# A four-layer decoder on one core: at which results of the second mixture GpSimd takes the context norm's two powers

## The chip, the core and the metric

The kernel runs on one core of a Trainium2 chip. The metric is the device time of one launch in microseconds (us), the median of several runs. The core has TensorE (matrix products, written PE in the profile), VectorE (DVE), ScalarE (ACT), GpSimd (POOL), SyncE (SP), which issues most transfers, and 16 DMA engines. Each engine works its own list of instructions in order and waits on semaphores that the others raise.

## The reference, cut to what matters

Twelve residual sublayers follow each other: self-attention, cross-attention and a feed-forward part, in four layers. The change stands in the sixth, a mixture of 8 experts with two choices for each of the 1024 tokens, and concerns the eighth, whose context norm is worked out ahead of time in the sixth.

```python
x = x + _L1_ffn_ref(_layernorm(x, axis=-1), L1_ffn_gate_w, L1_ffn_w1, L1_ffn_w2, L1_ffn_w3)
x = x + _L2_attn_ref(_layernorm(x, axis=-1), L2_attn_Wqkv...)
x = x + _L2_xattn_ref(ctx_1024, mask_BxS2_bf1, _layernorm(x, axis=-1), L2_xattn_gm, L2_xattn_bm,
                      L2_xattn_gl, L2_xattn_bl, L2_xattn_Wq, L2_xattn_Wk, L2_xattn_Wv, L2_xattn_Wo)

def _layernorm(x, gamma, beta):          # of the eighth sublayer, for its context of 4 x 512 rows
    mu = jnp.mean(x, axis=-1, keepdims=True)
    var = jnp.var(x, axis=-1, keepdims=True)
    return (x - mu) * jax.lax.rsqrt(var + EPS) * gamma + beta
```

(The second line is abridged: its arguments are the sublayer's weights and biases.)

## The kernel before

**The mixture.** The tokens' choices are packed into 23 blocks of 128 rows, each with one expert. For every block b, TensorE makes the two up products (lines L1993 and L1995), ScalarE the SiLU of the first (L2064, tile `gated`), VectorE the product of both (L2260), TensorE the down product (L2006), and VectorE copies the result y(b) out of PSUM (L2267). In TensorE's list the down product of block b-1 stands behind the up products of block b. The up products of block b wait for VectorE's product of block b-2, and the down product of b-1 for that of b-1. So in VectorE's list, step b is: product of block b, copy of result b-1, and then, for b from 2 to 19, one step of the context's norm.

**The context's norm** is taken in two halves of 8 tiles of 128x128 (tile `qs`), nine steps each (`CTX_STEPS = 9`). Steps 0 to 3 take statistics, two tiles each; step 3 ends with `veps` (L3091). Step 4 is empty. Step 5 waits for `rstd`, which GpSimd makes from `veps` with one power (L279), and steps 5 to 8 scale two tiles each (L3097). The first half's veps comes in VectorE's step b = 5 and is wanted as rstd in its step b = 7; the second half's in b = 14, wanted in b = 16.

**GpSimd's list** in this mixture is short: eight gathers of token rows for blocks 4 to 11 (L2341, scr_h to the row buffer, which the profile calls `probs`), then for each b the scatter of result y(b) to DRAM (L2329, `scr_y`), behind it for b from 4 to 14 the gather for block b + 8, and at two values of b the power. The sizes that tie the engines are these: results have 8 buffers, and VectorE's copy of y(b), b from 8 on, waits until the scatter of y(b-4) has landed; rows have 8 buffers, two blocks a group, and TensorE turns a group (L1980) just ahead of the up products of the odd block before it. So TensorE turns blocks 12 and 13 ahead of block 11's up products.

**SyncE** loads an expert's weights (768 KB, L1784) into one of 5 buffers; the load for block b waits for the down product of block b-5. When all scatters have landed, it fetches the results back (L1801), and VectorE adds them to x (L2305). TensorE meanwhile starts on the eighth sublayer's keys (L2967 to L2983).

Of the kernel before, what the change touches and what calls it, by code (L numbers as in the profile page):

```python
# [79 lines left out]
def program(nc, a, ctx):  # L80
# [190 lines left out]
    def norm_gpsimd(pool, n, first=0):  # L271
        for part in range(first, parts_of(n)):
            power_gpsimd(pool, n, part)
# [85 lines left out]
    class Attention:  # L359
# [1172 lines left out]
        def gpsimd(self, pool):  # L1532
            for who, what, s, u in self.order():
                who.gpsimd_step(pool, what, s, u)
# [119 lines left out]
    CTX_STEPS = 9  # L1654

    class Mixture:
# [655 lines left out]
        def gpsimd(self, pool):  # L2312
            m = self.m
            if self.sorted:
                pool.wait_ge(placed.sem, placed.at(m, 2))
                pool.wait_ge(written, 16 * 7)
                for t in range(self.choices * NT):
                    pool.indirect_dma_start(scr_x, bass.IndirectOffsetOnAxis(ap=place[:, t:t + 1], axis=0),
                                            h[:, t % NT, :], None).then_inc(sorted_out.sem, 16)
                pool.wait_ge(mapped.sem, mapped.at(m, 1))  # L2320
            else:
                pool.wait_ge(h_spill.sem, h_spill.at(m, 4))
                pool.wait_ge(mapped.sem, mapped.at(m, 1))
                for b in range(self.turned_in * self.gb, self.turned_in * self.gb + RING):
                    self.gather_gpsimd(pool, b)
            pool.wait_ge(mapped.sem, mapped.at(m, 2))
            for b in range(self.nb):
                pool.wait_ge(y_sb.sem, y_sb.at(m, b + 1))
                pool.indirect_dma_start(scr_y, bass.IndirectOffsetOnAxis(ap=scatter_to[:, b:b + 1], axis=0),  # L2329
                                        yblk[:, self.at(b), :], None).then_inc(y_spill[b % 4].sem, 16)  # L2330
                if not self.sorted and self.turned_in * self.gb <= b < self.nb - RING:
                    self.gather_gpsimd(pool, b + RING)
                if m == 1 and b in (6, 6 + CTX_STEPS):
                    norm_gpsimd(pool, 7 + b // CTX_STEPS)

        def gather_gpsimd(self, pool, b):
# [1403 lines left out]
```

## Time and profile before

| | us |
|---|---|
| median of 3 runs | 1364.19 (1357.69 to 1368.22) |
| profiled execution | 1358.5 |
| its span, first to last instruction | 1356.7 |
| TensorE busy in the span | 1195.5 (88%) |
| VectorE | 898.5 (66%) |
| ScalarE | 733.3 (54%) |
| GpSimd | 272.9 (20%) |

The span is what the trace covers; the 1.8 us beside it lie before the first and after the last instruction. A share of busy time is a mean over twelve sublayers with different limits, so it doesn't tell what bounds one of them. All times in the rows are counted from the start of the span. The blocks of the changed mixture lie between about 462 and 535 us.

### The profile page before, as it was taken

The numbers are of one execution on the slowest core, as the hardware profiler recorded it, in microseconds if no ns is written. First come the engines' busy times: TensorE is split into PE (matmuls) and PEld (weight loads), VectorE is DVE, ScalarE is ACT, GpSimd is POOL, SyncE is SP. The second block draws the span as 40 slices with busy tenths as digits, with TensorE's granted clock in tenths as the row PEclk, the third lists the DMA queues.
The fourth block names the chain that finished last, engine by engine and source line by source line (L and its number), as shares of the span: only waits on it lengthen the run. The fifth ranks groups of instructions, "written<-read, shape, count | busy, mean of one in ns | idle before, by whom it ended". The sixth has DMA issues, their size and how long they took to land.

```text
span 1356.7 us, 26928 instructions
## 1 busy us (share of the span) xinstructions
PE 1195.5 (88%) x9641; PEld 723.5 (53%) x9641; DVE 898.5 (66%) x2346; ACT 733.3 (54%) x1501; POOL 272.9 (20%) x562
## 2 busy tenths in 40 slices
PE   5888999896887899669999999999988968989995
PEld 2334343793343598455666666666656833333333
DVE  4767995445767543776766676777746176777866
ACT  3565884232733323545666666676734535646674
POOL 2521220562010174210000000000005505212220
PEclk9898999998997899899999999999989989989997
DMA  7431238563412586300000000011116734211200
GB/s 175 114 72 46 57 122 325 202 219 119 116 41 74 186 278 205 124 1 1 1 1 1 1 1 1 9 33 47 40 42 210 251 125 108 62 48 50 54 9 16
DMA packets 90180, 121.69 MB, mean 90 GB/s; under 512 B 10977, under 2 KB 68014, under 8 KB 89070
## 3 DMA queue, kind: packets, MB, share of 16 engines
q1 hardware_dynamic: 84322, 110.40, 26.3%
q0 software_dynamic: 4096, 8.40, 1.9%
q8 instruction: 79, 1.29, 0.4%
q10 hardware_dynamic: 1632, 1.18, 0.3%
q14 instruction: 51, 0.42, 0.1%
HBM read 88.94 MB, written 30.02 MB: 88 GB/s over the span
## 4 chain that ended last, share of the span: by engine, by line
PE 65%; DVE 14%; ACT 5%; DMA 5%; issue 5%; POOL 3%; SPq 2%; DVEq 0%; ACTq 0%; POOLq 0%
PE ps L2910 7%; PE ps L2917 7%; PE ps L2925 6%; PE ps L1202 6%; PE ps L945 4%; PE ps L1993 3%; PE ps L2006 3%; PE ps L954 3%; PE ps L2999 3%; PE ps L3006 2%; PE ps L1995 2%; PE ps L1112 2%; PE ps L1239 2%; PE ps L231 2%; PE ps L1902 2%
## 5 line engine op out<-in xcount | busy, mean ns | idle before, releaser
L3117 DVE CUSTOM_DVE_ANT_0 wring<-ps,probs 128x768 f32<-128x768 f32 x128 | 122.6, 958 | 46.1 <-PE ps L2910 45.4
L3076 ACT COPY qs<-ps 128x768 f32<-128x768 f32 x128 | 102.3, 800 | 90.3 <-PE ps L2917 90.3
L1202 PE MATMUL ps<-probs,vaug 128*32 128x256 f32 (+1 forms) x1792 | 142.3, 392 | 5.0 <-issue 3.5
L1157 ACT ACTIVATE probs<-ps 128x512 f32<-128x512 f32 x192 | 104.2, 595 | 60.0 <-PE ps L998 59.8
L279 POOL TENSOR_TENSOR rstd<-veps,mhalf 128x4 f32<-128x4 f32 (+2 forms) x28 | 26.6, 949 | 514.6 <-DVE veps L247 501.3
L1030 DVE TENSOR_REDUCE mx<-ps 128x2 f32<-128x1024 f32 (+1 forms) x96 | 115.5, 1220 | 22.1 <-PE ps L945 21.2
L1161 ACT ACTIVATE probs<-ps 128x512 f32<-128x512 f32 x192 | 104.7, 594 | 39.2 <-PE ps L1112 38.0
L3057 ACT ACTIVATE wring<-wring,r 128x768 f32<-128x768 f32 x128 | 120.8, 944 | 3.9 <-DVE r L3120 3.9
L2917 PE MATMUL ps<-ident,wring 128*128 128x128 f32 x768 | 110.2, 280 | 3.2 <-DVE wring L3161 3.2
L2917 PEld LDWEIGHTS ps<-ident,wring 128*128 128x128 f32 x768 | 83.4, 140 | 41.9 <-issue 35.3
L2910 PE MATMUL ps<-probs 64*128 64x512 f32 (+1 forms) x512 | 100.4, 510 | 1.1 <-DVE r L3117 1.1
L2329 POOL DMA_INDIRECT scr_y<-probs x85 | 82.1, 966 | 70.2 <-DVE probs L2267 53.5
L1018 DVE CUSTOM_DVE_ANT_0 wring<-ps,m3x 128x512 f32<-128x512 f32 x128 | 83.2, 688 | 17.0 <-PE ps L945 9.7
L2925 PE MATMUL ps<-qs,ks 128*64 128x256 f32 x768 | 89.9, 383 | 0.0
L3161 DVE TENSOR_SCALAR wring<-wring,r 128x768 f32<-128x768 f32 x128 | 79.4, 621 | 4.5
L945 PE MATMUL ps<-ks,qs 49*128 49x256 bf16 (+1 forms) x512 | 76.9, 338 | 4.6 <-DVE mx L1030 1.8
L2260 DVE TENSOR_TENSOR probs<-gated,ps 128x256 f32<-128x256 f32 (+1 forms) x62 | 32.2, 520 | 58.6 <-ACT gated L2064 32.7
L2064 ACT ACTIVATE gated<-ps 128x256 f32<-128x256 f32 (+1 forms) x62 | 28.7, 463 | 76.6 <-PE ps L1995 76.6
L2910 PEld LDWEIGHTS ps<-probs 64*128 64x128 f32 x512 | 44.4, 187 | 47.6 <-issue 40.9
L2925 PEld LDWEIGHTS ps<-qs,ks 128*64 128x64 f32 x768 | 52.3, 137 | 28.4 <-issue 5.2
L1202 PEld LDWEIGHTS ps<-probs,vaug 128*32 128x32 f32 x1792 | 36.7, 109 | 52.2 <-issue 47.7
L1112 PE MATMUL ps<-qs,ks 52*128 52x256 bf16 x384 | 54.5, 281 | 4.7 <-DMA qs<-mT 2.9
(397 smaller groups left out, 2468.1 us busy)
## 6 DMA issues: line engine op xcount, KB each, us to landing
wring<-in_L_ffn_w SPq DMA_DIRECT2D x21, 768.0 KB, 5.5
wring<-in_L_ffn_w SPq DMA_DIRECT2D x19, 514.0 KB, 4.8
ks<-in_L_ffn_w SPq DMA_DIRECT2D x8, 768.0 KB, 14.5
qs<-in_L_ffn_w SPq DMA_DIRECT2D x6, 768.0 KB, 12.3
qs<-scr_q SPq DMA_DIRECT2D x18, 192.0 KB
qs<-scr_qx SPq DMA_DIRECT2D x16, 192.0 KB
probs<-scr_x SPq DMA_DIRECT2D x12, 256.0 KB, 5.4
probs<-in_L_ffn_w SPq DMA_DIRECT2D x4, 768.0 KB, 6.2
```

Of the source, the lines that this page charges most:

```text
L945: ins = pe.matmul(bank(at[r], i * self.keys, (i + 1) * self.keys), self.qv(s, c, r, ROWS_A, t * P, (t + 1) * P), self.kv(s, c, r, ROWS_A), ...
L1018: dve.tensor_tensor_reduce(wring[:, k % 2, r * S2:(r + 1) * S2], bank(self.banks(0, k)[r]), m3x[:, 0, a % 2 * S2:(a % 2 + 1) * S2], 1.0, - ...
L1030: dve.tensor_reduce(out, src, AX.X, ALU.max, negate=True).then_inc(a_max.sem, 1)
L1157: act.activation(probs[:, s % 2, 2 * c + r, kt0 * S:(kt0 + 2) * S], bank(self.banks(3, k)[r]), ACT.Exp).then_inc(p_exp.sem, 1)
L1161: act.activation(probs[:, s % 2, 2 * c + r, kt0 * S:(kt0 + 2) * S], bank(4 + k % 2), ACT.Exp).then_inc(p_exp.sem, 1)
L1202: ins = pe.matmul(ps[32 * j:32 * j + 32, self.av_bank(s), q0:S], vaug[:, s % 2, kt, j, :], probs[:, s % 2, j, at:at + S - q0], start=(kt = ...
L2910: ins = pe.matmul(bank(2 * j + lo // 512, 0, hi - lo), self.qT[rows, g % 2, k * P:(k + 1) * P], self.kT[rows, g % 3, lo:hi], start=True, s ...
L2917: ins = pe.transpose(self.buffer("turn", i, t * P, t * P + P), self.sc[:, i % 4, t * P:(t + 1) * P], ident[:, :])
L2925: ins = pe.matmul(self.buffer("sum", i, 0, S)[HW * j:HW * j + HW, :], self.v[:, i % 3, t, j * HW:(j + 1) * HW], self.pT[:, i % 2, j, t, :] ...
L3057: act.activation(self.sc[:, i % 4, :], self.sc[:, i % 4, :], ACT.Exp, bias=self.neg[:, i % 4:i % 4 + 1], accum_out=self.tot[:, i % 4:i % 4 ...
L3076: act.copy(self.pT[:, g % 2, j, :, k * P:(k + 1) * P], self.buffer("turn", i, 0, KV).rearrange("p (t n) -> p t n", n=P)).then_inc(self.out ...
L3117: dve.tensor_tensor_reduce(self.sc[:, s, :], src, self.maskb[:, u // (2 * PR), :], 1.0, -3.0e38, ALU.add, ALU.max, self.top[:, s:s + 1]).t ...
```

## The change

One line sets after which results GpSimd takes the two powers. Results are counted here from the first, y(0): the power of the first half moves from behind y(6) to behind y(3), that of the second half from behind y(15) to behind y(13).

```diff
                 if not self.sorted and self.turned_in * self.gb <= b < self.nb - RING:
                     self.gather_gpsimd(pool, b + RING)
-                if m == 1 and b in (6, 6 + CTX_STEPS):
+                if m == 1 and b in (3, 4 + CTX_STEPS):
                     norm_gpsimd(pool, 7 + b // CTX_STEPS)
```

`norm_gpsimd(pool, 7)` and `norm_gpsimd(pool, 8)` issue one power each:

```python
pool.wait_ge(ln_var.sem, ln_var.at(made(n), part + 1))
pool.tensor_tensor(rstd[:, at], veps[:, at], mhalf[:, at], ALU.pow).then_inc(ln_rstd.sem, 1)
pool.wait_ge(ln_rstd.sem, ln_rstd.at(made(n), part + 1))
```

No instruction is added or removed, and only GpSimd's list differs. Its first piece, at the head of the mixture's blocks (L2341 is a gather, L2329 a scatter of a result, L279 with 128x8 a power of the context's norm):

```order
 L2341 DMA probs<-scr_h,probs 128x128 x8
-L2329 DMA scr_y<-probs 7041x128 x5
-L2341 DMA probs<-scr_h,probs 128x128
-L2329 DMA scr_y<-probs 7041x128
-L2341 DMA probs<-scr_h,probs 128x128
-L2329 DMA scr_y<-probs 7041x128
-L2341 DMA probs<-scr_h,probs 128x128
+L2329 DMA scr_y<-probs 7041x128 x4
 L279 TENSOR_TENSOR rstd<-veps,mhalf 128x8
 L2329 DMA scr_y<-probs 7041x128
```

The power now stands behind four scatters in place of seven scatters and three gathers: the scatters of y(4), y(5), y(6) and the gathers for blocks 12, 13 and 14 come after it. The second piece, on GpSimd too, near the end of the blocks:

```order
 L2341 DMA probs<-scr_h,probs 128x128
 L2329 DMA scr_y<-probs 7041x128
+L2341 DMA probs<-scr_h,probs 128x128
+L2329 DMA scr_y<-probs 7041x128
+L2341 DMA probs<-scr_h,probs 128x128
 L279 TENSOR_TENSOR rstd<-veps,mhalf 128x8
-L2329 DMA scr_y<-probs 7041x128 x7
+L2329 DMA scr_y<-probs 7041x128
+L2341 DMA probs<-scr_h,probs 128x128
+L2329 DMA scr_y<-probs 7041x128 x8
```

Here the second power stands ahead of the scatters of y(14) and y(15) and of the last gather, for block 22, in place of behind them. (The plus lines above the power are those that the first power's move put behind it.)

## Rows read from the trace of the kernel before

**Rows 1.** The page: the span, and the chain that ended last, by engine.
```profile
span 1356.7 us, 26928 instructions
...
PE 65%; DVE 14%; ACT 5%; DMA 5%; issue 5%; POOL 3%; SPq 2%; DVEq 0%; ACTq 0%; POOLq 0%
```

**Rows 2.** Timeline of VectorE: start, length, instruction, and idle time before it.
```profile
481.51 0.17 DVE L3091 TENSOR_SCALAR veps<-mv 128x8 f32<-128x8 f32 x1
482.45 0.69 DVE L2260 TENSOR_TENSOR probs<-gated,ps 128x512 f32<-128x512 f32 x1 [0.77 <-ACT gated L2064]
...
492.01 0.60 DVE L3097 TENSOR_SCALAR qs<-qs,mv,rstd 128x128 f32<-128x128 f32 x2 [5.77 <-POOL rstd L279]
...
511.46 0.38 DVE L3091 TENSOR_SCALAR veps<-mv 128x8 f32<-128x8 f32 x1
...
519.18 0.60 DVE L3097 TENSOR_SCALAR qs<-qs,mv,rstd 128x128 f32<-128x128 f32 x2 [2.99 <-POOL rstd L279]
```

**Rows 3.** Timeline of TensorE in the mixture's blocks.
```profile
473.08 0.44 PE L1980 MATMUL ps<-ident,probs 128*128 128x128 f32 x2 [0.44 <-DMA probs<-scr_h,probs]
...
488.02 0.38 PE L1980 MATMUL ps<-ident,probs 128*128 128x128 f32 x2
...
493.26 1.62 PE L2006 MATMUL ps<-wring,probs 128*128 128x128 f32 x8 [3.07 <-DVE probs L2260]
```

**Rows 4.** Timeline of ScalarE: the SiLU of blocks 7, 8, 9, 10, 18, 19.
```profile
484.65 0.60 ACT L2064 ACTIVATE gated<-ps 128x512 f32<-128x512 f32 x1 [1.42 <-PE ps L1995]
487.33 0.60 ACT L2064 ACTIVATE gated<-ps 128x512 f32<-128x512 f32 x1 [2.08 <-PE ps L1995]
...
490.23 0.60 ACT L2064 ACTIVATE gated<-ps 128x512 f32<-128x512 f32 x1 [1.41 <-PE ps L1995]
497.87 0.60 ACT L2064 ACTIVATE gated<-ps 128x512 f32<-128x512 f32 x1 [7.04 <-PE ps L1995]
...
520.18 0.60 ACT L2064 ACTIVATE gated<-ps 128x512 f32<-128x512 f32 x1 [2.08 <-PE ps L1995]
...
523.63 0.60 ACT L2064 ACTIVATE gated<-ps 128x512 f32<-128x512 f32 x1 [1.42 <-PE ps L1995]
```

**Rows 5.** Timeline of GpSimd: two norms' powers, then scatters, a gather, the powers.
```profile
391.75 1.01 POOL L279 TENSOR_TENSOR rstd<-veps,mhalf 128x4 f32<-128x4 f32 x1 [0.37 <-DVE veps L247]
...
477.70 1.00 POOL L2329 DMA_INDIRECT scr_y<-probs  x1 [0.30 <-issue]
...
481.58 0.97 POOL L2329 DMA_INDIRECT scr_y<-probs  x1 [0.30 <-issue]
...
489.28 0.98 POOL L2341 DMA_INDIRECT probs<-scr_h,probs  x1 [0.30 <-issue]
490.29 1.68 POOL L279 TENSOR_TENSOR rstd<-veps,mhalf 128x8 f32<-128x8 f32 x1
...
517.47 1.68 POOL L279 TENSOR_TENSOR rstd<-veps,mhalf 128x8 f32<-128x8 f32 x1
```

**Rows 6.** Stretches: busy us by engine, then TensorE's granted clock, DMA share, GB/s.
```profile
493.20:497.20 4.00, 3.94 (x20) 3.94 (x21) 2.11 (x8) 0.00 (x0) 2.42 (x3) 0.57 0.23 46
...
472.50:476.50 4.00, 3.06 (x26) 2.71 (x25) 1.61 (x6) 0.79 (x2) 2.89 (x4) 1.00 0.84 210
...
479.00:488.00 9.00, 9.00 (x83) 9.00 (x82) 3.58 (x11) 2.76 (x5) 6.86 (x7) 1.00 1.01 342
503.00:527.00 24.00, 23.71 (x212) 23.52 (x211) 11.92 (x38) 6.86 (x13) 15.09 (x15) 1.00 0.95 306
```

**Rows 7.** DMA issues at 489.28, 516.47, 486.26, 495.63, 516.22: us to landing.
```profile
probs<-scr_h,probs POOLq DMA_INDIRECT x1, 4.6
...
scr_y<-probs POOLq DMA_INDIRECT x1, 6.7
...
wring<-in_L_ffn_w SPq DMA_DIRECT2D x1, 768.0 KB, 5.2
...
wring<-in_L_ffn_w SPq DMA_DIRECT2D x1, 768.0 KB, 4.6
...
wring<-in_L_ffn_w SPq DMA_DIRECT2D x1, 768.0 KB, 7.6
```

## The prediction

> **What bounds the kernel now.** I read the page's chain of waits first. TensorE holds 65% of the chain that ended last, and GpSimd only 3% [rows 1]; but the kernel is a row of sublayers, and one of them can hang on an engine that is idle elsewhere. So the second view is the timeline of the changed mixture, engine by engine. VectorE has its first veps ready at 481.51 + 0.17 = 481.68, and yet sits idle 5.77 us, up to 492.01, for the rstd made of it; the second time it idles 2.99 us, up to 519.18 [rows 2]. Why so late? GpSimd comes out of its eight gathers with four results already waiting and works without a pause from then on: from 477.70 to 489.28 lie nine intervals, so one transfer costs its queue 1.29 us. It reaches the power only at 490.29, 8.6 us after its input was there [rows 5, 2].
>
> Third, what the wait costs where it matters. VectorE's product of block 8 stands behind the waiting step. TensorE idles 3.07 us for it, then starts at 493.26 with a down product of 1.62 us, and in the stretch around it the granted clock is 0.57 on average, against 1.00 before [rows 3, 6]: after the idle time it works at the lower of its two levels (1.2 GHz of 2.4) for a while. The whole loss is best read on ScalarE, whose SiLU marks the end of each block's up products. Undisturbed they are 2.68 and 2.90 us apart in turn (487.33 - 484.65, 490.23 - 487.33), 5.58 us for two blocks. Block 10 should come at 490.23 + 2.68 = 492.91 and comes at 497.87 [rows 4]. **The first wait costs the chain 4.96 us**, some 3.2 as idle time and 1.7 as slow clock. The second wait: block 19 comes 3.45 us after block 18 (523.63 - 520.18) where 2.90 is the pace [rows 4]. **It costs 0.55 us**, since most of its 2.99 lie in VectorE's slack. Between and after them TensorE sets the pace of the blocks.
>
> **The change part by part.**
>
> *The first power, behind y(3).* GpSimd starts that scatter at 481.58 and is done at 482.55 [rows 5]; veps is there since 481.68, so the power doesn't wait, with 0.9 us to spare. It runs from 482.58 to 484.26 (1.68, the same shape as before [rows 5]). VectorE asks for rstd at 492.01 - 5.77 = 486.24 [rows 2], 2.0 us later: the wait of 5.77 is gone, and with it the loss of 4.96.
>
> *What is queued behind it.* y(4) is next. A power that waits for its own semaphore before the next instruction shows a gap of 0.37 [rows 5], so y(4) is issued at 484.63, against 481.58 + 1.29 = 482.87 before: 1.76 later. The gather of block 13 stands three transfers behind: 484.63 + 3 x 1.29 = 488.5. TensorE turned the group of blocks 10 and 11 at 488.02 [rows 3]; the group of 12 and 13 follows two blocks later, at 488.02 + 5.58 = 493.6, since TensorE no longer stops. The gather has 5.1 us to land. Its nearest neighbour, issued at 489.28, took 4.6; the slowest of GpSimd's transfers in these rows 6.7 [rows 7]. I take 4.6, thus no wait; the other end is 488.5 + 6.7 - 493.6 = 1.6 us. Each later group gains room, since two transfers a block cost GpSimd 2.58 us and a block lasts 2.79. VectorE's copy of y(8), at about 491.5, needs the scatter of y(4): 484.63 + 4.6 to 6.7 is 489.2 to 491.3, just in time, nothing.
>
> *The second power, behind y(13).* After the first power GpSimd lags: y(7), the fourth scatter from y(4) with three gathers between, goes at 484.63 + 6 x 1.29 = 492.4 and y(13), twelve transfers on, at 507.8; the gather behind it ends at 510.1, and the power at about 511.8. Its veps came at 511.46 + 0.38 before, now 4.96 us earlier, at 506.9. VectorE wants rstd at 519.18 - 2.99 - 4.96 = 511.2 [rows 2]. It still waits 0.6 us, well inside its slack (a wait of 2.99 cost 0.55), so the 0.55 us go too. The scatters of y(14) and y(15) and the last gather are some 2 us later than they would be; from y(16) on there are only scatters, GpSimd catches up, and the last one is issued when its result is copied, as before.
>
> *What is late next: the transfers.* A block moves 768 KB of weights and 64 KB each in and out, 0.9175 MB in 2.79 us, 329 GB/s. With the engines fully busy they moved 342 [rows 6]: little is left over. The stop of TensorE let them drain: the load issued after it landed in 4.6 us, the one before it had taken 5.2, and ten undisturbed blocks later, at 516.22, one took 7.6 [rows 7]. Block 20's up products end at 523.63 + 2.68 = 526.31 and take 1.99 (read from the undisturbed blocks: the SiLU at 490.23 follows the turn at 488.02 by 2.21, the turn itself 0.22), so its weights were wanted at 524.3, 8.1 us after the issue. Without the second stop that is 7.55. Without the first stop's pause the landing would be 0.6 longer (5.2 against 4.6), 8.2. I charge the difference, **0.6 us**. The ends: nothing, by the 342 GB/s, and 2.1 us by the 306 GB/s of the later stretch [rows 6]: ten blocks, 9.175 MB, in 30.0 us in place of 27.9.
>
> The Trainium skill ("DMA: Bandwidth & Descriptors", Where 436 GB/s comes from) puts the limit of HBM for one core at about 358 GB/s. By it the blocks' demand would always fit, and the sum would be the full 5.5; the trace is less generous, with landings that grow while the share stands near 1.
>
> *After the mixture* everything hangs on the last block: the scatters, the fetch back, the add to x and the next norm follow in a chain, and TensorE's work on the next keys starts when its blocks end. I find no transfer or engine there that runs on its own clock, so what is saved stays saved.
>
> **The sum:** -4.96 - 0.55 + 0.6 = **-4.9 us**. The profiled execution took 1358.5 us (a span of 1356.7 and 1.8 around it) and would take 1353.6. The median of the runs shown is 5.7 us above that execution; from it, 1364.2 - 4.9 = **1359.3 us**, 0.4% less.
>
> **The rivals.**
>
> *The transfers take most of it back.* For it: the share near 1 and the landings of 6.7 and 7.6. Against it: the waits overlap (what TensorE loses at the turn it doesn't lose again at the weights), and the ring of five weight buffers has 2 us of room. With both ends, 1.6 at the turn and 2.1 at the weights, 1.8 us of gain are left: 1362.4; in the middle, 1361.
>
> *The power is held up at its new place.* Both powers of before ran while VectorE stood idle; now VectorE has a product of 0.69 us from 482.45 on [rows 2]. If the power can't run beside it, the power and all behind it come up to 0.6 us later, the gather of block 13 at 489.1 lands at 493.7 to 495.8, and up to 2.2 us are lost at the turn: from -4.8 to -3.3, middle 1360. The Trainium skill ("SBUF — State Buffer", Who interferes with whom) has such a rule: a VectorE instruction with two SBUF inputs and a GpSimd instruction that reads SBUF exclude each other. This product reads one input from PSUM, so the rule speaks only weakly here.
>
> *It does nothing.* If the end of the mixture hung on something that the trace's waits don't name, the time would stay: 1364.2. TensorE's idle time names VectorE's product, and that product stands directly behind the wait; I see little room.
>
> *Slower.* GpSimd's list is strict, and three gathers now stand behind the power. If the gather of block 13 landed so late that TensorE idled over 3.8 us at the turn, the clock would fall as it did after 3.07 us and cost 1.7 more, and the sum turns positive. That needs a landing of 8.9 us or more; at 10 us it is 4.9 + 1.7 - 5.5 = +1.1, 1365.3. The slowest of GpSimd's transfers in the rows took 6.7 [rows 7]. A short idle alone doesn't lower the clock: it stayed at 1.00 around the 0.44 us before 473.08 [rows 3, 6].
>
> **How the numbers follow.** The forecast 0.65 (-5.5 to -4.0), transfers 0.18, held power 0.06, nothing 0.06, slower 0.02, and 0.03 for more than forecast, should later stretches at the lower clock fall shorter. About 1% is what a measurement of this kernel can tell from no change; it is 13.6 us here, and no case reaches it by its mechanism. What is left for the other two is scatter: the three runs lie within 10.5 us. Faster by over 1% 0.05, within 1% 0.93, slower 0.02. The mechanisms span 1358.7 to 1364.2; half the scatter, 5.3, to either side makes 1353.4 to 1369.5. The profiled execution as the basis gives a time 5.7 lower, so I move the range down: 1350 to 1366.
>
> **What the changed profile would show.** VectorE's first L3097 with no wait on rstd, and the second with under 1 us; the SiLUs of blocks 8 to 22 at 2.68 and 2.90 throughout, and no granted clock of 0.5 around 495; the first 128x8 power near 482.6; block 19's SiLU near 518.1 (523.63 - 5.51) or up to 0.6 later. It would be wrong if TensorE waited for rows at the turn near 493.6 or for weights from block 16 on, if the power waited for veps, or if the mixture ended 5 us earlier and a later sublayer gave it back.

## The result, and the profile after

The changed kernel takes 1358.66 us (median of 22 runs, 1349.83 to 1364.93), against 1368.3 us for the kernel before in 22 runs beside it. The ratio is 0.995, with a 95% interval of 0.9929 to 0.9972: 0.5% faster, or 7 us of some 1366. The profiled execution took 1362.48 us with a span of 1360.7.

That span is 4.0 us longer than that of before [rows 1], so the page alone would mislead. Its first line and its chain by engine:

```profile
span 1360.7 us, 26923 instructions
...
PE 66%; DVE 13%; DMA 6%; ACT 5%; issue 5%; POOL 2%; SPq 2%; DVEq 0%; ACTq 0%; POOLq 0%
```

GpSimd's share of the chain went from 3 to 2%, that of the transfers from 5 to 6%. To see what the change did, the two traces have to be laid side by side at the mixture. ScalarE's SiLU of block 0 starts at 464.15 before and at 468.17 here: 4 us have been lost ahead of the change, in sublayers that it doesn't touch. I therefore count every kernel from block 0's SiLU to block 22's. **That stretch took 67.63 us before and takes 63.22 now, 4.41 less.**

The timeline of VectorE in the changed kernel (start, length, instruction, idle time before it), to be read beside [rows 2]:

```profile
485.30 0.17 DVE L3091 TENSOR_SCALAR veps<-mv 128x8 f32<-128x8 f32 x1
486.24 0.69 DVE L2260 TENSOR_TENSOR probs<-gated,ps 128x512 f32<-128x512 f32 x1 [0.77 <-ACT gated L2064]
...
489.94 0.59 DVE L3097 TENSOR_SCALAR qs<-qs,mv,rstd 128x128 f32<-128x128 f32 x2
...
516.24 0.79 DVE L3097 TENSOR_SCALAR qs<-qs,mv,rstd 128x128 f32<-128x128 f32 x2
```

Neither of the two L3097 that follow a power has idle time any more, where 5.77 and 2.99 us stood. GpSimd's timeline, beside [rows 5]:

```profile
485.58 0.97 POOL L2329 DMA_INDIRECT scr_y<-probs  x1 [0.30 <-issue]
486.57 1.69 POOL L279 TENSOR_TENSOR rstd<-veps,mhalf 128x8 f32<-128x8 f32 x1
488.55 1.02 POOL L2329 DMA_INDIRECT scr_y<-probs  x1 [0.29 <-POOL rstd L279]
...
492.47 0.98 POOL L2341 DMA_INDIRECT probs<-scr_h,probs  x1 [0.30 <-issue]
...
514.01 1.68 POOL L279 TENSOR_TENSOR rstd<-veps,mhalf 128x8 f32<-128x8 f32 x1
```

The first power begins 1.1 us after its veps and ends at 488.26, before VectorE asks. The gather of block 13 goes out at 492.47. ScalarE's SiLUs of blocks 9, 10, 11 and of 18, 19, beside [rows 4]:

```profile
494.02 0.60 ACT L2064 ACTIVATE gated<-ps 128x512 f32<-128x512 f32 x1 [1.41 <-PE ps L1995]
496.70 0.60 ACT L2064 ACTIVATE gated<-ps 128x512 f32<-128x512 f32 x1 [2.08 <-PE ps L1995]
...
500.90 0.60 ACT L2064 ACTIVATE gated<-ps 128x512 f32<-128x512 f32 x1 [1.41 <-PE ps L1995]
...
520.32 0.60 ACT L2064 ACTIVATE gated<-ps 128x512 f32<-128x512 f32 x1 [2.08 <-PE ps L1995]
...
523.21 0.60 ACT L2064 ACTIVATE gated<-ps 128x512 f32<-128x512 f32 x1 [1.42 <-PE ps L1995]
```

Block 9 to 10 is 2.68 us (7.64 before), block 18 to 19 is 2.89 (3.45 before). But block 10 to 11 is 4.20, where 2.90 is the pace: 1.30 us are new. TensorE's timeline and two stretches (busy us by engine, granted clock, DMA share, GB/s) say what they are:

```profile
498.64 0.44 PE L1980 MATMUL ps<-ident,probs 128*128 128x128 f32 x2 [1.09 <-DMA probs<-scr_h,probs]
```
```profile
493.20:497.20 4.00, 4.00 (x38) 4.00 (x38) 1.44 (x5) 1.10 (x2) 3.09 (x4) 1.00 0.96 328
...
497.00:500.00 3.00, 1.91 (x17) 1.73 (x17) 1.40 (x4) 0.67 (x2) 2.26 (x3) 1.00 0.97 314
```

TensorE waits 1.09 us for the token rows of blocks 12 and 13 at their turn. The granted clock stays at 1.00 through it (0.57 in the stretch 493.20:497.20 of [rows 6]), and no other turn and no load of weights is waited for from there on. So the balance is -4.96 - 0.56 + 1.30, and -0.19 of small differences at blocks 3 to 5 and beyond: -4.41.

### The profile page after: what moved, and what is told of

Same layout as the page of the kernel before. It is cut to its first block, busy times and chain, and to the rows that moved or that the text cites. A ratio compares the mean times of both kernels' runs of the same rounds, so it can differ in the third digit from the quotient of the medians.

```text
span 1360.7 us, 26923 instructions
## 1 busy us (share of the span) xinstructions
PE 1201.9 (88%) x9636; PEld 727.5 (53%) x9641; DVE 898.9 (66%) x2346; ACT 734.4 (54%) x1501; POOL 271.5 (20%) x562
## 4 chain that ended last, share of the span: by engine, by line
PE 66%; DVE 13%; DMA 6%; ACT 5%; issue 5%; POOL 2%; SPq 2%; DVEq 0%; ACTq 0%; POOLq 0%
PE ps L2910 7%; PE ps L2917 7%; PE ps L2925 6%; PE ps L1202 6%; PE ps L945 4%; PE ps L1993 3%; PE ps L2006 3%; PE ps L954 3%; PE ps L2999 3%; PE ps L3006 2%; PE ps L1112 2%; PE ps L1995 2%; PE ps L231 2%; PE ps L1239 2%; PE ps L1902 2%
## 5 line engine op out<-in xcount | busy, mean ns | idle before, releaser
L279 POOL TENSOR_TENSOR rstd<-veps,mhalf 128x4 f32<-128x4 f32 (+2 forms) x28 | 26.6, 949 | 519.4 <-DVE veps L247 506.0
L2329 POOL DMA_INDIRECT scr_y<-probs x85 | 81.9, 964 | 67.2 <-DVE probs L2267 47.5
```

## The experiments

Each was read in two ways: by the stretch from block 0's to block 22's SiLU in its trace, which differs by 0.06 to 0.24 us in the three kernels that were traced twice, and by its runs against the kernel before, whose intervals are 6 to 10 us wide in all. The stretch is one trace each, so differences of a few tenths say nothing.

| kernel | blocks 0 to 22, us | ratio to before | 95% interval |
|---|---|---|---|
| before | 67.63 | | |
| before again (e10) | 67.40 | 1.0016 | 0.998 to 1.0052 |
| changed | 63.22 | 0.995 | 0.9929 to 0.9972 |
| changed again (e5) | 63.28 | 0.9952 | 0.9926 to 0.9978 |
| first power alone (e1) | 64.00 | 0.9985 | 0.9962 to 1.0009 |
| second power alone (e2) | 67.38 | 1.0005 | 0.9979 to 1.0031 |
| norm steps two blocks later (e3) | 62.11 | 0.9956 | 0.9932 to 0.9981 |
| the same again (e11) | 62.35 | 0.9923 | 0.9891 to 0.9956 |
| one more power (e4) | 64.71 | 0.9983 | 0.9959 to 1.0007 |
| two more powers (e8) | 65.12 | 0.9994 | 0.9969 to 1.0019 |
| gather ahead of scatter (e6) | 64.27 | 0.9945 | 0.9916 to 0.9974 |
| first power behind y(5) (e7) | 62.85 | 0.9956 | 0.9927 to 0.9984 |
| lighter loads (e9) | 61.41 | 0.9933 | 0.9902 to 0.9965 |

**e1: only the first power moves** (from the kernel before).

```diff
-                if m == 1 and b in (6, 6 + CTX_STEPS):
+                if m == 1 and b in (3, 6 + CTX_STEPS):
```

> Only the power of the first half moves, behind y(3); the second stays behind y(15). My theory: VectorE's first wait (5.77 us) is gone and TensorE's stop and slow clock of 4.96 us with it, TensorE waits about 1.1 us at the turn of blocks 12 and 13, as in the changed kernel, and at the second power GpSimd's backlog costs VectorE a wait of 2 to 4 us, of which 0.4 to 1.5 us reach TensorE. From block 7 to block 22, ScalarE's SiLUs take 3.0 to 4.0 us less than before. Rival, that the gain needs both moves: the second wait grows by as much as the first shrank, and the mixture ends within 1.5 us of before.

The blocks take 64.00 us, 3.63 less than before. VectorE's one wait for rstd, and TensorE's two waits:

```profile
520.47 0.60 DVE L3097 TENSOR_SCALAR qs<-qs,mv,rstd 128x128 f32<-128x128 f32 x2 [3.23 <-POOL rstd L279]
```
```profile
499.56 0.44 PE L1980 MATMUL ps<-ident,probs 128*128 128x128 f32 x2 [0.93 <-DMA probs<-scr_h,probs]
...
521.72 1.16 PE L2006 MATMUL ps<-wring,probs 128*128 128x128 f32 x8 [0.53 <-DVE probs L2260]
```

The first wait is gone without the second move; the second is 3.23 us in place of 2.99 and lets block 19 come 0.79 us late. The rival is out. The wait for rows at 499.56 belongs to the first move.

**e2: only the second power moves.**

```diff
-                if m == 1 and b in (6, 6 + CTX_STEPS):
+                if m == 1 and b in (6, 4 + CTX_STEPS):
```

> Only the power of the second half moves, behind y(13). My theory: the first wait stays at 5.5 to 6 us with its slow clock, the second goes from 3.0 to under 0.7 us, and the blocks gain 0.4 to 0.7 us. Rival, that most of the 8 us between the two kernels' runs comes from the second half or from a later sublayer that wants it early: a gain of 2 us or more.

67.38 us, 0.25 less than before, where 0.4 to 0.7 were expected; of the two waits for rstd one is left. VectorE, and TensorE's down product behind it:

```profile
486.69 0.60 DVE L3097 TENSOR_SCALAR qs<-qs,mv,rstd 128x128 f32<-128x128 f32 x2 [6.15 <-POOL rstd L279]
```
```profile
487.94 2.08 PE L2006 MATMUL ps<-wring,probs 128*128 128x128 f32 x8 [3.45 <-DVE probs L2260]
```

Block 18 to 19 is 2.90 here, so the 0.55 us are won. Block 19 to 20, at 3.10, gives 0.4 back: TensorE waits for the weights of block 20.

```profile
518.63 0.49 PE L1993 MATMUL ps<-probs,wring 128*128 128x128 f32 x2 [0.16 <-DMA wring<-in_L_ffn_w]
```

The first wait costs 0.25 us more than in the trace of before. The second move does what it should and weighs little, and nothing large hides in it.

**e10: the kernel before, again.**

> The kernel before, once more, for its scatter: the runs differ from the kernel before itself by nothing beyond their interval, VectorE waits 5.5 to 6.3 us for the first rstd and 2.8 to 3.3 for the second, and the blocks take 67.2 to 68.0 us. Rival, that the first wait is often far longer than in the profile shown, which would explain a difference of 8 us between the runs: over 69 us.

The same two waits as in [rows 2 and 3], 5.92 and 2.99 us, and 67.40 us in all; the ratio to itself, 1.0016, shows what the runs can tell:

```profile
494.57 0.60 DVE L3097 TENSOR_SCALAR qs<-qs,mv,rstd 128x128 f32<-128x128 f32 x2 [5.92 <-POOL rstd L279]
521.55 0.60 DVE L3097 TENSOR_SCALAR qs<-qs,mv,rstd 128x128 f32<-128x128 f32 x2 [2.99 <-POOL rstd L279]
```

The rival, a first wait that is often far longer, has no support: three traces with the power behind y(6) show 5.77, 5.92 and 6.15 us.

**e5: the changed kernel, again.**

> The changed kernel once more, beside the next three. From block 0's to block 22's SiLU the traces gave 67.63 us before and 63.22 changed, 4.41 less, while the means of the two kernels' runs lay 8.2 apart. My theory: the blocks are all that changed and the rest is scatter; here the blocks take 62.9 to 63.6 us, TensorE waits 0.7 to 1.5 us for rows at the turn of blocks 12 and 13, and the runs lie 3 to 7 us under those of before. Rival, that a later sublayer gains too: 8 us or more again.

63.28 us, with 1.11 us of waiting for rows at the same turn. The means of the runs lie 5.5 us apart (standard error 1.3), against 8.2 (1.35) in the first comparison: together 6.8, with a standard error of 0.9. The rival, 8 us or more again, has no support.

**e3 and e11: leave the powers, move who asks.** From the kernel before, VectorE takes the norm's steps two blocks later.

```diff
-                if m == 1 and 2 <= b < 2 + 2 * CTX_STEPS:
-                    others[7].context_vector(dve, *divmod(b - 2, CTX_STEPS))
+                if m == 1 and 4 <= b < 4 + 2 * CTX_STEPS:
+                    others[7].context_vector(dve, *divmod(b - 4, CTX_STEPS))
```

> Both powers stay where they were, behind y(6) and y(15), and VectorE takes its eighteen steps of the context's norm two blocks later (b from 4 to 21). Both rstd are then made when VectorE asks for them. My theory (the changed kernel's wait at the turn comes from GpSimd's list, which issues the gather of block 13 1.8 us later): no wait of VectorE over 0.4 us, the gather of block 13 goes 2.6 us ahead of that of block 14 and TensorE waits under 0.3 us at its turn; the blocks take 5.2 to 5.8 us less than before, about 1.1 less than changed. Rival, that the full transfer engines make that wait, whatever GpSimd does: TensorE waits 0.8 us or more at that turn or at a neighbouring one, and nothing is won against the changed kernel.

62.11 us, 5.52 less than before, and the gap of every block from 4 on is 2.68 to 2.99. One wait of 0.20 us for rstd is left, and no turn is waited for:

```profile
495.76 0.60 DVE L3097 TENSOR_SCALAR qs<-qs,mv,rstd 128x128 f32<-128x128 f32 x2 [0.20 <-POOL rstd L279]
```

> VectorE's norm steps two blocks later, once more. The first time the blocks took 62.11 us with no wait at any turn or for weights. My theory (the gather of block 13 has room when it stands ahead of the power): 62.0 to 62.6 us again. Rival, that this was luck with the transfer engines, which cost the kernel with the gathers ahead of the scatters 2.2 us in waits for weights: over 63 us.

62.35 us; nothing at the turn of blocks 12 and 13 this time either, only 0.42 us between blocks 7 and 8. Those 0.42 us are a wait for the weights of block 8. Against the two traces of before, the two of this kernel give 5.1 to 5.5 us by another way than the changed one. At the same pace of the blocks, its gather of block 13 goes out 6.9 us ahead of the turn (5.1 in the changed kernel) and lands after 4.9, so the pace as such doesn't make the 1.3 us.

**e7: the first power behind y(5) and its gather** (from the changed kernel).

```diff
-                if m == 1 and b in (3, 4 + CTX_STEPS):
+                if m == 1 and b in (5, 4 + CTX_STEPS):
```

> The first power behind y(5) and its gather, the second behind y(13) as in the changed kernel. The gathers of blocks 12 and 13 then go out before the power. My theory: VectorE waits 2.6 to 3.4 us for rstd, of which its slack hides all but 0.3 to 0.8, and TensorE doesn't wait at the turn: 62.4 to 62.9 us for the blocks, better than changed. Rival, that the wait at the turn isn't tied to the order of gather and power: it is there as well, and the blocks take over 63.6.

62.85 us, 0.4 under the changed kernel. VectorE waits, TensorE less, and there is no wait for rows:

```profile
495.10 0.60 DVE L3097 TENSOR_SCALAR qs<-qs,mv,rstd 128x128 f32<-128x128 f32 x2 [3.55 <-POOL rstd L279]
```
```profile
496.35 1.16 PE L2006 MATMUL ps<-wring,probs 128*128 128x128 f32 x8 [0.85 <-DVE probs L2260]
```

Both the wait and its cost are above what was expected (2.6 to 3.4 us, and 0.3 to 0.8). 3.55 us of waiting cost 1.12 at the next block (3.80 against 2.68), where 5.77 cost 4.96: the price of this wait is far from proportional. VectorE's slack hides a part, and the granted clock stayed at 1.00 after the stop of 0.85.

**e6: the gather ahead of the scatter** (from the changed kernel).

```diff
+                if not self.sorted and self.turned_in * self.gb <= b < self.nb - RING:
+                    self.gather_gpsimd(pool, b + RING)
                 pool.indirect_dma_start(scr_y, ...)
-                if not self.sorted and self.turned_in * self.gb <= b < self.nb - RING:
-                    self.gather_gpsimd(pool, b + RING)
```

> The changed kernel, with GpSimd's gather for block b + 8 ahead of the scatter of y(b) in place of behind it. My theory: the gather of block 13 is issued 1.3 us earlier, TensorE's wait at the turn falls from 1.1 to under 0.3 us, and the blocks take 62.0 to 62.5 us against 63.2; the scatter of y(4) is 1.3 us later and may hold VectorE's copy of y(8) by up to 0.5 us. Rival, that loaded transfer engines make the wait: it stays at 0.8 us or more.

The wait for rows is gone, as my theory had it, but the blocks take 64.27 us: TensorE waits for the weights of blocks 8, 19 and 20.

```profile
484.33 0.49 PE L1993 MATMUL ps<-probs,wring 128*128 128x128 f32 x2 [0.93 <-DMA wring<-in_L_ffn_w]
...
515.80 0.49 PE L1993 MATMUL ps<-probs 128*128 128x128 f32 x2 [0.41 <-DMA probs<-in_L_ffn_w]
...
519.23 0.49 PE L1993 MATMUL ps<-probs,wring 128*128 128x128 f32 x2 [0.49 <-DMA wring<-in_L_ffn_w]
```

The waits sum to 1.83 us, and these three blocks come 2.6 us later than at the pace. The size expected was missed by 1.8 us. The stop at block 8 also gave the gather of block 13 another 1.2 us; since it landed after 5.1 us, it would have been in time without it. It can't be said from one trace whether the new order made these waits: e4 waits 1.34 us for block 8's weights too, and of the two traces of the same kernel, e3 and e11, only the second does.

**e4 and e8: hold up GpSimd more** (from the changed kernel). One or two further powers behind the first, on a spare tile. The edit of e4:

```diff
                     norm_gpsimd(pool, 7 + b // CTX_STEPS)
+                if m == 1 and b == 3:
+                    pool.tensor_tensor(spare_pow[:, :], mhalf[:, :], mhalf[:, :], ALU.pow)
```

> The changed kernel with one more power of 128x8 on GpSimd, right behind the first one, whose result nobody reads: it holds up GpSimd's list by some 1.7 us and VectorE not at all. My theory: the gather of block 13 lands that much later, TensorE's wait at the turn grows from 1.1 to 2.6 to 3.0 us, the later groups wait too or get by with little room, and the blocks take 1.5 to 2.0 us more than in the changed kernel. Rival, that the wait is made by the transfer engines: it stays within 0.7 us of 1.1. If the clock falls after that wait as it did after 3.07 us, another 1 to 1.7 us are lost.

64.71 us, 1.49 over the changed kernel. But the wait at the turn, expected at 2.6 to 3.0 us, is as before, and 1.34 us went elsewhere:

```profile
489.32 0.49 PE L1994 MATMUL ps<-probs,wring 128*128 128x128 f32 x2 [1.34 <-DMA wring<-in_L_ffn_w]
...
498.85 0.44 PE L1981 MATMUL ps<-ident,probs 128*128 128x128 f32 x2 [1.01 <-DMA probs<-scr_h,probs]
```

(Lines are one further down in this kernel.) The wait for weights comes first and covers the delay, so this kernel alone decides nothing. Hence the doubling:

> The changed kernel with two further powers of 1.63 us behind the first one, whose results nobody reads: GpSimd's list is held up by 3.3 us more than in the changed kernel. With one such power a wait of 1.34 us for weights stood ahead of the turn and hid what it did there. My theory: the waits of TensorE for rows and those that come from VectorE's copies waiting for scatters sum to 1.1 + 3.3 = 4.4 us, give or take 0.8; if one of them is over 3 us the granted clock falls to about half and 1 to 1.7 us are lost besides. The blocks take 66.5 to 68.5 us, as many as before the change. Rival, that the list has room: they take under 65.

65.12 us, against 66.5 to 68.5 expected. GpSimd's extra powers, the gather of block 13, and then TensorE's and VectorE's waits:

```profile
487.18 3.23 POOL L2338 TENSOR_TENSOR spare_pow<-mhalf 128x8 f32<-128x8 f32 x2
...
494.51 0.97 POOL L2345 DMA_INDIRECT probs<-scr_h,probs  x1 [0.31 <-issue]
```
```profile
498.70 0.44 PE L1981 MATMUL ps<-ident,probs 128*128 128x128 f32 x2 [1.33 <-DMA probs<-scr_h,probs]
```
```profile
495.79 0.29 DVE L2268 COPY probs<-ps 128x128 f32<-128x128 f32 x1 [0.57 <-DMA scr_y<-probs]
498.58 0.29 DVE L2268 COPY probs<-ps 128x128 f32<-128x128 f32 x1 [0.68 <-DMA scr_y<-probs]
```

**Here my theory fell.** Counted from block 0's SiLU, the gather of block 13 went out 3.2 us later than in the changed kernel. TensorE came to the turn 1.0 us later, for stops that lie ahead of the extra powers, and waited only 0.2 us longer. The gather landed 4.2 us after its issue; in the changed kernel TensorE could go on 6.2 us after it (492.47 to 498.64). So the wait isn't GpSimd's lateness passed on. What GpSimd's transfers did in the changed kernel shows in four single microseconds, from 492, 493, 495 and 496 on (queue, packets, MB, time of its packets as a share of 16 engines):

```profile
q1 hardware_dynamic: 55, 0.33, 88.3%
q0 software_dynamic: 3, 0.00, 1.1%
...
q1 hardware_dynamic: 63, 0.31, 75.4%
q0 software_dynamic: 32, 0.08, 20.6%
...
q1 hardware_dynamic: 58, 0.36, 93.3%
...
q1 hardware_dynamic: 57, 0.28, 92.5%
q0 software_dynamic: 41, 0.09, 23.1%
```

q0 is GpSimd's queue, q1 that of the weights. In the microsecond from 495 on no packet of GpSimd moves at all, though two of its transfers are on their way; then 41 in the next. Rows come in bursts among the weights.

**e9: the changed kernel with a third of the weights left out.**

```diff
+                w = 1024 if m == 1 and b >= WS else n
-                sp.dma_start(wslot[b % WS][:, 0:n], self.packed[bass.ds(expert, 1), :, :]...
+                sp.dma_start(wslot[b % WS][:, 0:w], self.packed[bass.ds(expert, 1), :, 0:w]...
```

> The changed kernel, but from block 5 on only the first two thirds of an expert's weights are loaded (512 KB in place of 768; the down products use what an earlier expert left, so this part of the computation is left out). GpSimd's list is as in the changed kernel. The traces so far: TensorE waits 1.1 to 1.3 us at the turn of blocks 12 and 13 whether the gather of block 13 goes out as in the changed kernel, 1.7 or 3.3 us of queue later, and GpSimd's packets run in bursts between the weights'. My theory now: the gather has to get past the weights in the transfer engines, and its lateness only decides in which burst it goes. With a third of the weights gone it lands in under 4.5 us, the wait at the turn is under 0.2 us, and the blocks take 61.7 to 62.2 us. Rival, that GpSimd's lateness alone makes the wait: it stays at 0.8 us or more.

61.41 us, 0.3 less than expected, and block 10 to 11 is 2.94: 1.26 of the 1.81 us against the changed kernel are won there, and 0.52 between blocks 3 and 4. GpSimd's list stands as in the changed kernel (the gather of block 13 at 492.62); its DMA issue, and a stretch of the blocks:

```profile
probs<-scr_h,probs POOLq DMA_INDIRECT x1, 4.3
```
```profile
484.00:496.00 12.00, 12.00 (x110) 12.00 (x109) 6.11 (x20) 3.13 (x6) 9.55 (x10) 1.00 0.77 240
```

With the DMA engines 77% busy the gather lands in 4.3 us and TensorE doesn't wait. All traces together, for the gather of block 13 (room is from its issue until TensorE comes to the turn):

| kernel | room, us | landing, us | wait, us |
|---|---|---|---|
| changed, e5, e1 | 5.1 to 5.3 | 6.1 to 6.2 | 0.93 to 1.11 |
| e4 | 5.1 | 6.1 | 1.01 |
| e8 | 2.9 | 4.2 | 1.33 |
| e9 | 4.4 | 4.3 | none |
| e3, e6, e7, e11 | 6.9 to 7.7 | 4.9 to 5.3 | none |

The wait came wherever the room was about 5 us or less at full loads, and was absent in each of the four traces with 6.9 us or more. What sets the landing time is only partly shown. e9 says fewer weights, but in e8 the gather landed in 4.2 us with the DMA engines 94% busy meanwhile, and in e4 in 6.1 with 87%. So e9 can owe its 4.3 us to its lighter loads or to where the gather fell among them. One thing the traces do show. A transfer's semaphore is raised in 16 steps. In each of the four traces that took 6.1 to 6.2 us, 15 of the 16 had come 5.0 to 5.4 us after the issue and the last one alone came 0.8 to 1.2 us behind them: most of the wait at this turn is for the slowest sixteenth of one gather.

## Why the prediction was right, and where it was off

**The first power.** Right: block 9 to 10 lost the 4.96 us, idle time and slow clock together. That it agrees to the hundredth is luck, since the same wait cost 4.93 and 5.21 us in e10 and e2. The power ran without waiting for veps. e1 shows that this move alone brings 3.63 of the 4.41 us.

**What is queued behind it.** Here the working went wrong. The issue times were right (the scatter of y(4) came 2.97 us after that of y(3), predicted 3.05; the gather of block 13, 3.9 behind it), and so was the room of 5.1 us. The step that failed is "Its nearest neighbour, issued at 489.28, took 4.6" and "I take 4.6, thus no wait". It took 6.1 to 6.2 and cost 1.30, near the other end, 1.6. The neighbour was on its way mostly while TensorE stood still, and behind the load issued at 488.98 came none until 495.63; in the changed kernel the loads go on. The row was the nearest in time, but not in what surrounded it. The trace of before had others: its gathers of blocks 8 and 9, issued at 472.70 and 473.95 with TensorE at work for most of the time, took 5.7 and 6.3 us. With 6.3 the same sum gives 488.5 + 6.3 - 493.6 = 1.2 us, nearly what was measured.

**The second power.** Its 0.55 us went (0.56). The wait of 0.6 us that I expected at 511.2 didn't occur, since TensorE's stop at the turn gave GpSimd 1.3 us. In e9, without that stop, VectorE does wait, 1.22 us, and block 19 is on time all the same: that it would lie in VectorE's slack was right.

**The transfers.** The 0.6 us charged at the weights of block 20 were not lost there: no load was waited for in either trace of the changed kernel. In e2 and e6 block 20's weights did come late, by 0.4 and 0.75 us, and block 8's in e4, e6 and e11, so this wait comes and goes. The working also says that the ring of weight buffers "has 2 us of room"; its own rows, wanted after 8.1 us and landed after 7.6, leave 0.5. The resource was named rightly, but not the place.

**The sum.** Predicted -4.9, measured in the trace -4.41; up to VectorE's first add to x it is -4.7 (77.71 us from block 0's SiLU before, 73.02 now). Two errors in it lean against each other: 1.30 us at the turn that it had at nothing, and 0.6 us at the weights that weren't lost. The predicted 1359.3 us and the measured 1358.7 agree better than the argument deserves: the kernel before took 1368.3 us beside the changed one, 4.1 above the 1364.2 that I started from, and the medians were 9.6 apart where I forecast 4.9.

**The rivals.** The blocked power didn't happen: it started when the scatter ahead of it was issued and took 1.69 us beside a busy VectorE, 1.68 beside an idle one. The transfers took back a quarter of the gain, not most of it. "It does nothing" and "slower" are out: the ratio's interval ends at 0.9972, and the blocks are 4.1 to 4.4 us shorter in all four pairs of traces. Even with two further powers in GpSimd's list (e8) the stop at the turn stayed at 1.33 us, the clock at its full level, and the blocks took 2.3 to 2.5 us less than before.

**What stays open.** Why the gather's last sixteenth comes so late in four traces and not in e8 isn't known. The runs of the two comparisons give 6.8 us with a standard error of 0.9, the traces 4.4 to 4.7. And in two traces each, the rest of the program, from that add to the end, took 814.8 and 819.2 us before and 819.5 and 816.5 changed: no gain shows there, and a scatter of 5 us would hide one of 2. Whether another 2 us are real isn't settled.

## What to carry to other kernels

A short job on a lightly loaded in-order engine can stop the busiest one. What counts is what stands ahead of it in its list when its result is wanted. Its place should be bounded from both sides: late enough for its input, early enough for its reader, and not ahead of transfers whose room is about their landing time. When a stall is removed, the transfers that ran in its shadow lose their quiet, so their landing has to be taken from a stretch where all goes on at full pace. Moving the reader can do as well or better: taking the norm's steps two blocks later (e3, e11) gave 62.1 and 62.35 us where the changed kernel takes 63.2.

## What the runs showed of the hardware

- The landing of GpSimd's gathers isn't its issue time plus a constant: for the same one, 6.1 us in the changed kernel, 4.2 when issued 3.2 us later (e8), 4.3 with a third less weight traffic (e9). Where it took longest, one of its 16 parts came 0.8 to 1.2 us behind the others.
- The Trainium skill ("DMA: Bandwidth & Descriptors", SWDGE vs HWDGE vs iDMA) says that GpSimd's transfers and those of the other engines use different queues inside a DMA engine, which takes them in turn. In the changed kernel both queues move packets in most microseconds, which agrees, but not evenly: in the one from 495 on it shows none of GpSimd's packets, and 41 in the next.
- A stop of TensorE of 3.07 to 3.45 us (before, e10, e2) was followed by a down product of 1.62 to 2.08 us in place of 1.06, with the granted clock at 0.5. After stops of 0.85 to 1.34 us (e7, changed, e4, e8) the granted clock stayed at 1.00.
- The Trainium skill ("SBUF — State Buffer", Who interferes with whom) names pairs of instructions in which GpSimd and VectorE exclude each other, and says that a VectorE instruction with at most one input in SBUF, outside of certain fast modes, isn't among them. The power beside VectorE's product, whose other input is in PSUM, agrees: 1.69 against 1.68 us.
- GpSimd's indirect transfers, issued one behind the other, mostly start 1.24 to 1.31 us apart in the changed kernel's blocks: 0.94 to 1.00 us for the instruction itself and 0.30 between two.
